# Gathered rows in five slots instead of three, gathers four tile steps ahead, attention steps written out

## The chip, the core and the metric

One NeuronCore of a Trainium2 chip runs the whole program in one launch. The metric is the device time of that launch in microseconds. The core's engines each run their own list of instructions in order and meet at semaphores: TensorE (PE), VectorE (DVE), ScalarE (ACT), GpSimd (POOL) and SyncE (SP). DMAs are issued by SP, ACT and POOL; only POOL issues those with row indices.

## The reference

32 batches of 128 tokens, 512 wide, pass a block of gated cross-attention and a gated mixture of experts.

```python
x = x + tanh(g_xattn) * attention(layernorm(x), ctx, ctx)      # 32 query heads, 8 key heads, depth 16
h = layernorm(x)
logits = tanh(h @ Wg1.T) @ Wg2.T                               # 8 experts
top_idx = top_k(logits, 2); scores = softmax of the two, else 0
out = sum over e of scores[e] * (silu(h @ Wup[e].T + bup[e]) @ Wdown[e].T + bdown[e])
x = x + tanh(g_ffn) * out
```

The output is x, in float32.

## The kernel before, in words

**Attention stage.** A software pipeline over the 32 batches. In step s an engine works on several batches at once: it normalises batch s-1, scores batch s-2, and so on to the placement of batch s-7. The function pipeline runs steps 0 to 11 written out, steps 12 to 23 inside a register loop of each engine (Fori, four steps in an iteration, three iterations), and the rest written out. VectorE's statistics of a new batch (L1055) stand once in each step. At the end of a batch its tokens are ranked within their two experts, and GpSimd scatters the normalised rows by two indirect DMAs (L656) to the experts' regions in DRAM.

**Expert stage.** The scattered rows form 71 tiles of 128 rows, each of one expert (TILES). Tile t passes several tile steps: loaded by ACT's queue (z_s), transposed (L1379), multiplied up (L1398 to L1400), activated, multiplied down (L1410 to L1412), its bias added by VectorE in out_rows (L1112) into one of two buffers y_sb, and stored by SP to expert_out in DRAM (L384). out_rows(t) runs in VectorE's tile step t+4 and waits until the store of tile t-2 has landed.

**Mixing.** A token's output needs two rows of expert_out, from the tiles of its two experts. Batch m is mixed at tile step MIX[m], by a formula: at earliest LAG = 9 steps after the tiles that hold its rows, and 1.5 steps after batch m-1. From batch 24 on these steps are 68, 69, 72, 73, 76, 77, 80, 81; batches 24 and 25 need tiles up to 58, 26 and 27 up to 62, 28 and 29 up to 66, 30 and 31 up to 70, the last. The work on a batch goes in this order:

- GpSimd gathers the batch's rows by two indirect DMAs of 256 KB (gather, L695), first y2 and then y1, into slot m % YRING. Before the first batch of a group of two it waits until the group's tiles are stored (stored_through), and before each gather until the slot's earlier batch is used up.
- ACT scales y2 (L846), VectorE multiplies y1 and adds y2 (L1155), GpSimd adds the sum to the residual r_in (L707), and SP stores the result (L377).
- For the last four batches (LATE) VectorE does all of it (L1128, L1132).

GpSimd's list is written by tile steps, and in step s it first holds the adds of the batches with MIX = s-2 and then the gathers of those with MIX = s+2. Nothing but its waits ties it to the tile steps of other engines. Its list near the end is then: add 24, gather 26, add 25, gather 27, add 26, gather 28, add 27, gather 29, gather 30, gather 31. SP's list has, by tile steps, the store of tile s-4, then the stores of mixed batches with MIX = s-3, then loads of residuals.

Of the kernel before, what the change touches and what calls it, by code (L numbers as in the profile page):

```python
# [51 lines left out]
EPS = 1e-5  # L52
TAB0 = 24
UP = 12582912.0
LOOP1 = 24
O_LOAD, O_NORM, O_S, O_ST, O_OUT, O_GATE, O_ROUTE, O_SLOT = range(8)
STEPS = B + O_SLOT
SOLO = B - 1 + O_GATE
LOOP0 = 12
YRING = 3  # L60
RRING = 5
LAG = 9
RING = 4
# [11 lines left out]
        eng.wait_ge(sem, value)  # L75


def pipeline(eng, step, steps, first, last, unroll):

    for s in range(first):  # L80
        step(s, s % unroll)
    with eng.Fori(0, (last - first) // unroll) as i:
        for u in range(unroll):
            step(i * unroll + (first + u), (first + u) % unroll)
    for s in range(last, steps):
        step(s, s % unroll)


# [24 lines left out]
def mixed_at(s):  # L113

    return [m for m in range(B) if MIX[m] == s]


def block_kernel(nc, x_d, ctx_d, gx_d, gf_d, wg1_d, wg2_d, w_d, bup_d, bdn_d, out_d):
# [5 lines left out]
    with top:  # L124
# [182 lines left out]
        def ring4(b, q, per):  # L307

            return (b - q) * (per // 4) + per
# [6 lines left out]
        @block.sync  # L316
        def _(sp):
            def first_tiles():

                for b in range(SEG[0] - RING, SEG[0]):  # L320
                    sp.wait_ge(scattered[b % RING], ring4(b, b % RING, 32))
                sp.wait_ge(tab_in[0], 32)
                for t in range(RING):
                    row = sp.value_load(tab_r[0:1, t:t + 1], min_val=0, max_val=ROWS - P)
                    sp.dma_start(z_s[t][:, :], slots_d[bass.ds(row, P), :]).then_inc(tile_loaded[t], 16)

            def step(s, u):
                if isinstance(s, int) and s == SOLO:
                    sp.wait_ge(pv_done, 2 * B)
                    sp.wait_ge(on_done, 2 * B)  # L330
                    sp.dma_start(bdn[:, :], bdn_d.to_broadcast([P, E * D])).then_inc(bdn_loaded, 16)
                b, p = s - O_LOAD, (u - O_LOAD) % 2
                if valid(b):
                    wait(sp, n_done, b - 1)
                    sp.dma_start(x_in[p][:, :], x_d[bass.ds(b, 1), :, :].rearrange("a s d -> (a s) d")).then_inc(x_loaded[p], 16)
                    wait(sp, kt_done, b - 1)
                    wait(sp, v_done, b - 1)
                    sp.dma_start(c_in[p][:, :], ctx_d[bass.ds(b, 1), :, :].rearrange("a s d -> (a s) d")).then_inc(c_loaded[p], 16)
                b, p = s - O_OUT, (u - O_OUT) % 2
                if valid(b):  # L340
                    wait(sp, z_done, b - 1)
                    wait(sp, res_stored[p], ring2(b - 2, p))
                    sp.dma_start(x_res[p][:, :], x_d[bass.ds(b, 1), :, :].rearrange("a s d -> (a s) d")).then_inc(res_loaded[p], 16)
                b = s - O_LOAD
                if valid(b):
                    wait(sp, w_lo_done, b)
                    sp.dma_start(wst[:, :], w_d[bass.ds(b, 1), :, :].rearrange("a p n -> (a p) n")).then_inc(w_loaded, 16)
                b, p = s - O_GATE, (u - O_GATE) % 2
                if valid(b):
                    sp.wait_ge(res_done, b + 1)  # L350
                    sp.dma_start(x2_d[bass.ds(b, 1), :, :].rearrange("a s d -> (a s) d"), x_res[p][:, :]).then_inc(res_stored[p], 16)


                if isinstance(s, int) and s == SOLO - 2:
                    sp.wait_ge(w_lo_done, B)
                    sp.wait_ge(n_done, B)
                    sp.wait_ge(kt_done, B)
                    sp.wait_ge(v_done, B)
                    sp.wait_ge(qt_done, B)
                    sp.dma_start(bup[:, :], bup_d.to_broadcast([P, E * HE])).then_inc(bup_loaded, 16)  # L360
                    first_tiles()

            pipeline(sp, step, SOLO + 1, LOOP0, LOOP1, RING)

            def load_residual(m):

                wait(sp, stored[m % RRING], 16 * (m // RRING))
                sp.dma_start(r_in[m % RRING][:, :], x2_d[m:m + 1, :, :].rearrange("a s d -> (a s) d")
                             ).then_inc(r_loaded[m % RRING], 16)

            def store_mixed(m):

                if m < LATE:
                    sp.wait_ge(mix2, m + 1)
                else:
                    sp.wait_ge(late_done, m - LATE + 1)
                sp.dma_start(out_d[m:m + 1, :, :].rearrange("a s d -> (a s) d"), r_in[m % RRING][:, :]  # L377
                             ).then_inc(stored[m % RRING], 16)

            for s in range(TSTEPS):  # L380
                t, p = s - 4, s % 2
                if valid(t, TILES):
                    sp.wait_ge(y_done, t + 1)
                    sp.dma_start(y_d[t * P:(t + 1) * P, :], y_sb[p][:, :]).then_inc(y_stored[p], 16)  # L384
                if s == 5:
                    sp.wait_ge(ends_done, 1)
                    sp.wait_ge(zero_done, 1)
                    _, found = nc.values_load_multi_w_load_instructions(
                        ends[0:1, :], engines=[mybir.EngineType.SP], min_val=0, max_val=ROWS - P,
                        skip_runtime_bounds_check_because="an expert's rows end within its region")  # L390
                    for row in found:
                        sp.dma_start(slots_d[bass.ds(row, P), :], r_in[0][:, :]).then_inc(pads_done, 16)
                if 20 <= s < 20 + RRING:
                    if s == 20:
                        sp.wait_ge(rows_done, 2)
                        scattered_all(sp)
                        sp.wait_ge(pads_done, 16 * E)
                        for b in range(B - 2, B):
                            sp.wait_ge(res_stored[b % 2], ring2(b, b % 2))
                    load_residual(s - 20)  # L400
                for m in mixed_at(s - 3):
                    store_mixed(m)
                for m in mixed_at(s - 6):
                    if m + RRING < B:
                        load_residual(m + RRING)
            for q in range(RRING):
                sp.wait_ge(stored[q], 16 * len(range(q, B, RRING)))

        @block.gpsimd
        def _(pool):  # L410
# [218 lines left out]
            def step(s, u):  # L629
# [10 lines left out]
                if valid(b5):  # L640
                    pool.wait_ge(res_loaded[p5_], ring2(b5, p5_))
                    pool.wait_ge(att_done, 2 * b5 + 2)
                    g.tensor_tensor(x_res[p5_][:, :], x_res[p5_][:, :], z[q5][:, :], ALU.add).then_inc(res_done, 1)  # L643
                    if isinstance(s, int) and TAB0 <= s < TAB0 + 11:
                        if s == TAB0:
                            pool.wait_ge(run_done, SEG[KNOWN - 1])
                        table(0, s - TAB0)
                    pool.wait_ge(o_mv, b5 + 1)
                    g.tensor_tensor(ve_o[:, :], mv_o[:, 1:2], eps[:, :], ALU.add).then_inc(o_ve, 1)
                    pool.wait_ge(o_ve, b5 + 1)  # L650
                    g.tensor_tensor(rs_o[:, :], ve_o[:, :], minus_half[:, :], ALU.pow).then_inc(o_rs, 1)
# [7 lines left out]
                if valid(b0):  # L659
# [2 lines left out]
                    g.tensor_tensor(ve_n[:, :], mv_n[:, 1:2], eps[:, :], ALU.add).then_inc(n_ve, 1)  # L662
                    pool.wait_ge(n_ve, b0 + 1)
                    g.tensor_tensor(rs_n[:, :], ve_n[:, :], minus_half[:, :], ALU.pow).then_inc(n_rs, 1)
                if isinstance(s, int) and s == SOLO:
                    pool.wait_ge(st_done[1], 2 * B)
                    pool.wait_ge(on_done, 2 * B)
                    g.memset(r_in[0][:, :], 0.0).then_inc(zero_done, 1)

            pipeline(pool, step, STEPS, LOOP0, LOOP1, RING)  # L670
            pool.wait_ge(run_done, B)
            for n in range(11):
                table(1, n)
# [27 lines left out]
            for s in range(TSTEPS):  # L701
                for m in mixed_at(s - 2):
                    if m >= LATE:
# [2 lines left out]
                    pool.wait_ge(mix1, m + 1)  # L706
                    g.tensor_tensor(r_in[m % RRING][:, :], r_in[m % RRING][:, :], y1[m % YRING][:, :],  # L707
                                    ALU.add).then_inc(mix2, 1)
                for m in mixed_at(s + 2):
                    if m == 0:  # L710
                        pool.wait_ge(rows_done, 2)
                    if m == 0 or m in SEG:
                        stored_through(tiles_through(level_of(m)))
                    gather(m, level_of(m))

        @block.scalar
        def _(act):
# [79 lines left out]
                    act.wait_ge(w_loaded, 16 * (s + 1))  # L797
                    a.activation(w_hi[:, bass.ds(s * WCHUNK, WCHUNK)], wst[:, :], ACT.Copy).then_inc(w_hi_done, 1)

            pipeline(act, step, SOLO, LOOP0, LOOP1, RING)  # L800

            def hidden(t):

# [65 lines left out]
        def _(dve):  # L869
# [192 lines left out]
                if valid(b6):  # L1062
                    masks(b6, p6_)

            pipeline(dve, step, SOLO, LOOP0, LOOP1, RING)

            expert = {}

# [142 lines left out]
        def _(pe):  # L1211
# [155 lines left out]
                    pe.wait_ge(att_done, 2 * b4 + 1)  # L1367
                    rows_back(b4, 1)

            pipeline(pe, step, SOLO, LOOP0, LOOP1, RING)  # L1370

            expert = {}

# [124 lines left out]
```

## Time and profile before

| | |
|---|---|
| runs shown | 698.03, 698.19, 696.45 us; median 698.03 |
| profiled execution | 695.72 us, of which span 693.9 us |
| TensorE matmul busy | 634.2 us, 91% of the span |
| VectorE busy | 521.6 us, 75% |
| ScalarE busy | 378.3 us, 55% |
| GpSimd busy | 353.8 us, 51% |
| granted TensorE clock, mean | 0.978 |
| moved by DMA | 129.40 MB, mean 186 GB/s |

The attention stage lasts until about 400 us, the expert stage from there to about 675 us, the mixing from about 510 us to the end. Shares of the whole span mix these stages; a stage has to be read by its own stretch, and the chain of waits says which engine's work ended last in it.

### The profile page before, as it was taken

What the parts mean: (1) busy time and instruction counts of PE and PEld (TensorE: products, weight loads), DVE (VectorE), ACT (ScalarE), POOL (GpSimd) and SP (SyncE); (2) the same over time, 40 slices, a digit from 0 to 9 for tenths busy, and PEclk for the clock granted to TensorE, in tenths of its full rate; (3) what the DMA queues carried; (4) which work ended last, traced back from release to release, by engine and by line L of the source; (5) the groups of instructions that cost most, each with busy time, mean ns of one, the idle gap of its engine ahead of it and who ended that gap; (6) DMA issues with size and microseconds to landing.
All of it is one profiled execution on the core that took longest, in us unless ns stands there. A gap on an engine that the chain in (4) does not pass through costs nothing.

```text
span 693.9 us, 17038 instructions
## 1 busy us (share of the span) xinstructions
PE 634.2 (91%) x5064; PEld 432.1 (62%) x5064; DVE 521.6 (75%) x1456; ACT 378.3 (55%) x692; POOL 353.8 (51%) x538
## 2 busy tenths in 40 slices
PE   3779999999999999999999977899999999999970
PEld 2435555555555555555555466789998888888850
DVE  3468888888888888888888455476767788887763
ACT  2267777777767676767676531333334544544430
POOL 4123545464545455656665536890032666575454
PEclk9999999999999999999999989899999999999995
DMA  3123344444444444444432677344665999999977
GB/s 103 53 66 116 114 141 149 139 142 141 144 140 144 140 144 141 145 141 145 143 126 77 208 279 256 109 154 152 215 227 177 304 348 345 348 354 352 334 250 256
DMA packets 65032, 129.40 MB, mean 186 GB/s; under 512 B 8640, under 2 KB 12736, under 8 KB 64704
## 3 DMA queue, kind: packets, MB, share of 16 engines
q1 hardware_dynamic: 44496, 77.35, 32.9%
q0 software_dynamic: 10368, 33.56, 14.3%
q10 hardware_dynamic: 10096, 17.59, 7.8%
q8 instruction: 38, 0.62, 0.4%
q14 instruction: 34, 0.28, 0.1%
HBM read 74.20 MB, written 54.26 MB: 185 GB/s over the span
## 4 chain that ended last, share of the span: by engine, by line
PE 77%; DVE 11%; issue 4%; DMA 2%; POOL 2%; ACT 1%; SPq 1%; DVEq 0%; ACTq 0%; POOLq 0%
PE s_ps L1281 13%; PE bank_a L1260 8%; PE st_ps L1304 8%; DVE nmax L993 7%; PE st_ps L1398 5%; PE st_ps L1399 5%; PE st_ps L1400 5%; PE s_ps L1379 4%; PE bank_c L1221 3%; PE bank_b L1269 3%; PE st_ps L1312 3%; PE bank_q L1356 2%; PE bank_a L1411 2%; PE bank_a L1412 2%; PE bank_a L1410 2%
## 5 line engine op out<-in xcount | busy, mean ns | idle before, releaser
L993 DVE TENSOR_REDUCE nmax<-s_ps 128x8 f32<-128x1024 f32 x128 | 156.4, 1222 | 62.3 <-PE s_ps L1281 61.2
L754 ACT ACTIVATE probs<-st_ps 128x1024 f32<-128x1024 f32 x128 | 131.2, 1025 | 67.2 <-PE st_ps L1312 63.6
L1281 PE MATMUL s_ps<-k_t,q_t 32*128 32x256 f32 x1024 | 151.9, 415 | 17.2 <-DVE nmax L993 14.4
L1304 PE MATMUL st_ps<-q_t,k_t 32*128 32x512 f32 x512 | 145.6, 645 | 0.3
L1281 PEld LDWEIGHTS s_ps<-k_t,q_t 32*128 32x128 f32 x1024 | 92.6, 192 | 68.9 <-DVE nmax L993 44.7
L695 POOL DMA_INDIRECT y<-expert_out,rows_all x64 | 64.6, 1009 | 57.7 <-DMA expert_out<-y_sb 43.3
L1398 PE MATMUL st_ps<-w_hi,zh 128*128 x284 | 86.9, 306 | 1.3 <-DVE zl L1092 1.3
L1399 PE MATMUL st_ps<-w_lo,zh 128*128 x284 | 80.7, 284 | 0.0
L1400 PE MATMUL st_ps<-w_hi,zl 128*128 x284 | 80.5, 283 | 0.0
L831 ACT ACTIVATE t_sb<-u_sb 128x256 f32<-128x256 f32 x71 | 29.7, 418 | 87.1 <-DVE u_sb L1102 78.1
L656 POOL DMA_INDIRECT slots<-z,slot_i x64 | 64.6, 1009 | 16.0 <-issue 15.7
L1260 PE MATMUL bank_a<-probs,v_aug 128*32 128x512 f32 x512 | 68.2, 605 | 0.0
L707 POOL TENSOR_TENSOR r_in<-r_in,y 128x512 f32<-128x512 f32 x28 | 36.4, 1299 | 59.1 <-DVE y L1155 57.1
L1398 PEld LDWEIGHTS st_ps<-w_hi,zh 128*128 128x128 f32 x284 | 55.0, 194 | 1.5 <-issue 1.5
L1399 PEld LDWEIGHTS st_ps<-w_lo,zh 128*128 128x128 f32 x284 | 55.4, 195 | 0.0
L1400 PEld LDWEIGHTS st_ps<-w_hi,zl 128*128 128x128 f32 x284 | 54.8, 193 | 0.0
L1092 DVE TENSOR_TENSOR zl<-s_ps,zh 128x512 fp32r<-128x512 f32 x71 | 49.1, 691 | 5.7 <-ACT zh L814 1.5
L643 POOL TENSOR_TENSOR x_res<-x_res,z 128x512 f32<-128x512 f32 x32 | 40.6, 1267 | 19.3 <-DVE z L892 19.3
L1312 PE MATMUL st_ps<-nm_t,pick 32*128 32x512 bf16 x256 | 49.1, 376 | 0.0
L761 ACT ACTIVATE o_sb<-bank_a 128x512 f32<-128x512 f32 x64 | 38.5, 602 | 16.1 <-PE bank_a L1260 16.1
L1379 PE MATMUL s_ps<-ident_f,z_s 128*128 128x128 f32 x284 | 43.3, 276 | 2.0 <-issue 1.8
L814 ACT ACTIVATE zh<-s_ps 128x512 fp32r<-128x512 f32 x71 | 42.2, 594 | 3.7 <-PE s_ps L1379 2.7
(182 smaller groups left out, 1376.6 us busy)
## 6 DMA issues: line engine op xcount, KB each, us to landing
expert_out<-y_sb SPq DMA_DIRECT2D x71, 256.0 KB, 3.9
z_s<-slots ACTq DMA_DIRECT2D x67, 256.0 KB, 3.9
x_in<-in_x SPq DMA_DIRECT2D x32, 256.0 KB, 2.7
wst<-in_w SPq DMA_DIRECT2D x32, 256.0 KB, 2.6
x_res<-in_x SPq DMA_DIRECT2D x32, 256.0 KB, 2.8
x_scratch<-x_res SPq DMA_DIRECT2D x32, 256.0 KB, 2.0
r_in<-x_scratch SPq DMA_DIRECT2D x32, 256.0 KB, 5.4
out<-r_in SPq DMA_DIRECT2D x32, 256.0 KB, 5.1
```

Of the source, the lines that this page charges most:

```text
L656: g.indirect_dma_start(out=slots_d, out_offset=bass.IndirectOffsetOnAxis(ap=slot_i[q7][:, j:j + 1], axis=0), in_=z[q7][:, :], in_offset=No ...
L695: g.indirect_dma_start(out=y[m % YRING][:, :], out_offset=None, in_=y_d[0:tiles_through(n) * P, :], in_offset=bass.IndirectOffsetOnAxis(ap ...
L754: a.activation(out, st_ps[:, :].rearrange("t (k n) -> t k n", k=2), ACT.Exp, scale=HD ** -0.5).then_inc(exp_done[half], 1)
L993: v.tensor_reduce(out, s_ps[:, :].rearrange("s (r g c t) -> s r g c t", r=2, g=2, c=2), X_AXIS, ALU.max, negate=True).then_inc(max_done, 1)
L1260: last = t_.matmul(bank_a[32 * j:32 * j + 32, :], v_aug[r][:, 32 * k:32 * k + 32], probs[:, k * G * S:(k + 1) * G * S], start=True, stop=True,
L1281: last = t_.matmul(s_ps[:, HALF * rr + 2 * P * gg:HALF * rr + 2 * P * (gg + 1)], q_t[r2][row:row + ROWS32, P * g_:P * (g_ + 1)], k_t[r2][r ...
L1304: t_.matmul(st_ps[:, HALF * rr:HALF * (rr + 1)], k_t[r][row:row + ROWS32, P * i:P * (i + 1)], q_t[r][row:row + ROWS32, :], start=True, sto ...
L1312: last = t_.matmul(st_ps[:, HALF * rr:HALF * (rr + 1)], pick[i][row:row + ROWS32, :], nm_t[p][row:row + ROWS32, :], start=False, stop=True ...
L1379: last = t_.transpose(bank[p][:, P * c:P * c + P], z_s[r][:, P * c:P * c + P], ident_f[:, :])
L1398: t_.matmul(o, zh[p][:, P * c:P * c + P], w_hi[:, cols], start=(c == 0), stop=False)
L1399: t_.matmul(o, zh[p][:, P * c:P * c + P], w_lo[:, cols], start=False, stop=False)
L1400: last = t_.matmul(o, zl[p][:, P * c:P * c + P], w_hi[:, cols], start=False, stop=(c == DC - 1))
```

## The change

YRING goes from 3 to 5, so the gathered rows y1 and y2 have five slots each. Four more buffers of 2 KB a partition are needed, and the scratch for dynamic transfers is set to 8192 bytes a partition. In GpSimd's list a batch's gathers stand in step MIX-4 instead of MIX-2. The register loops of all five engines go: pipeline writes every step out, and tests for a step's number lose their check of its type.

```diff
-LOOP1 = 24
-LOOP0 = 12
-YRING = 3
+YRING = 5
...
-def pipeline(eng, step, steps, first, last, unroll):
-
-    for s in range(first):
-        step(s, s % unroll)
-    with eng.Fori(0, (last - first) // unroll) as i:
-        for u in range(unroll):
-            step(i * unroll + (first + u), (first + u) % unroll)
-    for s in range(last, steps):
+def pipeline(step, steps, unroll):
+
+    for s in range(steps):
         step(s, s % unroll)
...
-            pipeline(pool, step, STEPS, LOOP0, LOOP1, RING)
+            pipeline(step, STEPS, RING)
...
-                for m in mixed_at(s + 2):
+                for m in mixed_at(s + 4):
                     if m == 0:
                         pool.wait_ge(rows_done, 2)
                     if m == 0 or m in SEG:
                         stored_through(tiles_through(level_of(m)))
                     gather(m, level_of(m))
...
-    nc = bacc.Bacc("TRN2", target_bir_lowering=False, num_devices=1)
+    nc = bacc.Bacc("TRN2", target_bir_lowering=False, num_devices=1, dynamic_dma_scratch_size=8192)
```

## Rows read from the trace of the kernel before

**Rows 1.** Timeline of VectorE: start us, us, engine, line, operation, out<-in, count.

```profile
70.67 0.68 DVE L1055 BATCH_NORM_STATS2 st_n<-x_in 128x6 f32<-128x512 f32 x1
...
128.28 0.69 DVE L1055 BATCH_NORM_STATS2 st_n<-x_in 128x6 f32<-128x512 f32 x1
...
279.98 0.68 DVE L1055 BATCH_NORM_STATS2 st_n<-x_in 128x6 f32<-128x512 f32 x1
...
360.63 0.69 DVE L1055 BATCH_NORM_STATS2 st_n<-x_in 128x6 f32<-128x512 f32 x1
```

**Rows 2.** Busy time by stretch: PE, PEld, DVE, ACT, POOL, clock, DMA share, GB/s.

```profile
480.00:500.00 20.00, 20.00 (x142) 18.11 (x142) 14.17 (x33) 7.68 (x18) 0.00 (x0) 1.00 0.60 202
...
560.00:580.00 20.00, 20.00 (x140) 17.92 (x139) 16.27 (x34) 10.21 (x22) 12.45 (x12) 1.00 1.00 343
...
680.00:700.00 20.00, 0.00 (x0) 0.00 (x0) 5.93 (x8) 0.00 (x0) 5.19 (x6) 0.60 0.51 168
```

**Rows 3.** Timeline of VectorE, L1112 (tiles 12, 16, 64, 65).

```profile
472.91 0.68 DVE L1112 SCALAR_TENSOR_TENSOR y_sb<-bank_q,bdn 128x512 f32<-128x512 f32 x1
...
486.68 0.68 DVE L1112 SCALAR_TENSOR_TENSOR y_sb<-bank_q,bdn 128x512 f32<-128x512 f32 x1
...
655.41 0.69 DVE L1112 SCALAR_TENSOR_TENSOR y_sb<-bank_q,bdn 128x512 f32<-128x512 f32 x1
...
659.64 0.69 DVE L1112 SCALAR_TENSOR_TENSOR y_sb<-bank_a,bdn 128x512 f32<-128x512 f32 x1 [0.72 <-DMA expert_out<-y_sb]
```

**Rows 4.** Waits, whole span: who waited for whom, us in total, times, longest us.

```profile
DVE r_in L1128 <- DMA y<-expert_out,rows_all: 7.1, 3, 4.8
...
DVE r_in L1132 <- DMA y<-expert_out,rows_all: 2.7, 3, 1.7
```

**Rows 5.** Chain of waits from 125 to 235 us: start us, us, what.

```profile
132.72 0.89 issue
...
226.48 0.89 issue
```

**Rows 6.** Timeline of GpSimd from 640 us (idle before and its releaser in brackets).

```profile
651.30 0.96 POOL L695 DMA_INDIRECT y<-expert_out,rows_all  x1
...
661.56 1.30 POOL L707 TENSOR_TENSOR r_in<-r_in,y 128x512 f32<-128x512 f32 x1 [5.48 <-DVE y L1155]
...
673.70 1.27 POOL L707 TENSOR_TENSOR r_in<-r_in,y 128x512 f32<-128x512 f32 x1 [4.44 <-DVE y L1155]
...
675.11 1.35 POOL L695 DMA_INDIRECT y<-expert_out,rows_all  x1
...
677.74 1.27 POOL L707 TENSOR_TENSOR r_in<-r_in,y 128x512 f32<-128x512 f32 x1
...
681.67 0.94 POOL L695 DMA_INDIRECT y<-expert_out,rows_all  x1 [0.30 <-issue]
...
685.77 0.95 POOL L695 DMA_INDIRECT y<-expert_out,rows_all  x1 [0.31 <-DVE r_in L1132]
```

**Rows 7.** Timeline of VectorE at the end.

```profile
674.27 0.69 DVE L1112 SCALAR_TENSOR_TENSOR y_sb<-bank_q,bdn 128x512 f32<-128x512 f32 x1 [0.72 <-PE bank_q L1412]
...
674.88 0.74 DVE L1155 SCALAR_TENSOR_TENSOR y<-y,coef 128x512 f32<-128x512 f32 x1
...
690.64 0.75 DVE L1132 SCALAR_TENSOR_TENSOR r_in<-y,coef,r_in 128x512 f32<-128x512 f32 x1 [0.50 <-DMA y<-expert_out,rows_all]
```

**Rows 8.** Timeline of SP's DMA queue at the end.

```profile
672.92 2.39 SPq L384 DMA_DIRECT2D expert_out<-y_sb  x2
```

**Rows 9.** DMA issues of the page: KB each, median us from issue to landing.

```profile
expert_out<-y_sb SPq DMA_DIRECT2D x71, 256.0 KB, 3.9
```

**Rows 10.** Chain of waits from 600 us to the end.

```profile
652.20 6.89 DMA expert_out<-y_sb
...
685.77 4.77 DMA y<-expert_out,rows_all
```

**Rows 11.** Tile expert_out, written by stores and read by gathers.

```profile
DMA to landing us min/median/max: 2.0/4.8/7.2
```

More of the change, by code:

```diff
@@ L327, in step @@
             def step(s, u):
-                if isinstance(s, int) and s == SOLO:
+                if s == SOLO:
                     sp.wait_ge(pv_done, 2 * B)
@@ L351, in step @@
                     sp.dma_start(x2_d[bass.ds(b, 1), :, :].rearrange("a s d -> (a s) d"), x_res[p][:, :]).then_inc(res_stored[p], 16)
-                if isinstance(s, int) and s == SOLO - 2:
+                if s == SOLO - 2:
                     sp.wait_ge(w_lo_done, B)
@@ L361, in step @@
                     first_tiles()
-            pipeline(sp, step, SOLO + 1, LOOP0, LOOP1, RING)
+            pipeline(step, SOLO + 1, RING)
             def load_residual(m):
@@ L643, in step @@
                     g.tensor_tensor(x_res[p5_][:, :], x_res[p5_][:, :], z[q5][:, :], ALU.add).then_inc(res_done, 1)
-                    if isinstance(s, int) and TAB0 <= s < TAB0 + 11:
+                    if TAB0 <= s < TAB0 + 11:
                         if s == TAB0:
@@ L664, in step @@
                     g.tensor_tensor(rs_n[:, :], ve_n[:, :], minus_half[:, :], ALU.pow).then_inc(n_rs, 1)
-                if isinstance(s, int) and s == SOLO:
+                if s == SOLO:
                     pool.wait_ge(st_done[1], 2 * B)
@@ L798, in step @@
                     a.activation(w_hi[:, bass.ds(s * WCHUNK, WCHUNK)], wst[:, :], ACT.Copy).then_inc(w_hi_done, 1)
-            pipeline(act, step, SOLO, LOOP0, LOOP1, RING)
+            pipeline(step, SOLO, RING)
             def hidden(t):
@@ L1063, in step @@
                     masks(b6, p6_)
-            pipeline(dve, step, SOLO, LOOP0, LOOP1, RING)
+            pipeline(step, SOLO, RING)
             expert = {}
@@ L1368, in step @@
                     rows_back(b4, 1)
-            pipeline(pe, step, SOLO, LOOP0, LOOP1, RING)
+            pipeline(step, SOLO, RING)
             expert = {}
```

## The prediction

> **What bounds the kernel now.** I read the busy time by stretch first, then the starts of one instruction that recurs in every step, then the waits, and last the chain with each engine's timeline at the end of the span. Three stages matter.
>
> In the attention stage TensorE and VectorE hand scores and maxima to each other, and a step takes the same time again and again. One mark per step is the statistics instruction of L1055 [rows 1]: from 70.67 to 128.28 there are five steps of 11.52 us; from 279.98 to 360.63 there are seven, again of 11.52 us. Between 128.28 and 279.98 lie 13 steps in 151.70 us. These are the steps that run inside the register loop (steps 12 to 23, and the entry into it). The reader is to see that only there the period is broken.
>
> In the expert stage TensorE is busy for 20.0 us of 20 both where the DMA engines are at 0.60 and where they are at 1.00 [rows 2]. The bias addition that ends a tile (L1112) starts at 472.91 for tile 12 and at 486.68 for tile 16: 3.44 us a tile [rows 3]. The gathers are not what anything waits for here: in the waits the only instructions that wait for gathered rows are the two of the last four batches, L1128 and L1132 [rows 4]. So a deeper look-ahead as such is worth nothing between 510 and 670 us, except through what it does to other transfers.
>
> At the end TensorE has stopped by 675 us, and 19 us follow in which a short chain runs: last tile written, stored, gathered, mixed, stored. In the last stretch VectorE and GpSimd are busy for 5.9 and 5.2 us [rows 2], so the tail is made of waits, and of GpSimd's one queue.
>
> **The change part by part.**
>
> *The loops.* The 13 marked steps took 151.70 us; at the undisturbed 11.521 us they take 149.78. Difference 1.92 us. The chain shows how it looks: pieces of 0.88 to 0.89 us called issue, the first at 132.72 and the last at 226.48, three in all and four steps (46.9 us) apart [rows 5], where the engines come to an iteration's start. Written out, these steps are like those on either side. Those are written out already and run at 11.52, so I take the whole 1.92 as gone. Bounds: 0 if the longer program is fetched no better than the loop was; 1.92 at most. Every later stage starts from this stage's end, so the gain is kept.
>
> *Queue order on GpSimd.* Steps are not clocked: GpSimd runs down its list as fast as waits let it. The batches from 24 on are mixed at steps 68, 69, 72, 73, 76, 77, 80, 81 (from the schedule's formula). With two steps of lead the list ends add 24, gather 26, add 25, gather 27, add 26, gather 28, add 27, gather 29, 30, 31. With four steps it is add 23, gather 26, 27, add 24, add 25, gather 28, 29, add 26, add 27, gather 30, 31. Five slots instead of three are what lets gather m go before add m-3 without waiting for its slot. The trace has the old order [rows 6]: add 24 at 661.56, add 26 at 673.70, gather 28 behind it at 675.11, add 27 at 677.74, then four gathers (29, 30) and the first of batch 30 at 681.67 behind the two of batch 29, the last of 31 at 685.77.
>
> *The tail.* The last tile's y_sb is written from 674.27 to 674.96, the mix of batch 27 ends at 675.62 [rows 7]; the store of that tile is the second of the two SP issues that end at 675.31 [rows 8], so it was issued at about 675.0. A store of this kind lands 3.9 us later in the median [rows 9]: 678.9. That is what gather 30 must have. In the old order it started at 681.67, because gathers 28 and 29 stood before it. In the new order they are long issued, and the queue is free once add 27 is done: 675.62 + 1.27 = 676.9. So gather 30 starts at 678.9, 2.7 us earlier. The three gathers behind it keep their 4.10 us (681.67 to 685.77), the last keeps its 4.77 us to landing [rows 10], the mix (690.64) and the last store keep theirs. Tail: -2.7 us. Bounds by the shortest and the longest landing of these transfers, 2.0 and 7.2 us [rows 11]: 677.0 gives -4.7, 682.2 gives +0.5. I take the median, since the DMA engines have less to do in that stretch once gathers 28 and 29 are out of it.
>
> The Trainium skill ("DMA: Bandwidth & Descriptors", Anatomy of one DMA) puts a GpSimd transfer at about 2.0 us plus its bytes over 436 GB/s, 2.6 us for 256 KB. The last gather's 4.77 us is far from that; by the page the sum would be 2.2 us better, by the trace it stays.
>
> *The wait that moves.* Gather 28 needs tile 66 in memory, and behind that wait now stand adds 26 and 27, and behind those SP's stores of the two batches. Tile 66 is written at 659.64 + 3.44 = 663.1, stored 0.7 later, landed 3.9 later: 667.7. Four gathers at 1.3 us end by 672.9; add 26 started at 673.70 anyway. With 7.2 us to landing they end at 676.2, adds 26 and 27 at 678.7: still before 678.9. Nothing is lost. Gather 26 needs tile 62, written at 655.41 - 2 x 3.44 = 648.5 and landed by 656.1 even at the 6.89 us seen below; add 24, which then stands behind gathers 26 and 27 (5 us), started at 661.56.
>
> *The late store.* One tile step takes 4.23 us (655.41 to 659.64), with 0.72 us of VectorE waiting for a y_sb buffer [rows 3]. The store it waited for took 6.89 us from 652.20 [rows 10]; two steps less the write of the buffer allow 2 x 3.44 - 0.69 = 6.19. Gather 25 was issued at 651.30 [rows 6], just ahead of it. In the new order gather 25 goes one batch earlier, behind add 21 instead of add 22, and the next one not before add 23. I take this 0.72 us as gone; bounds 0 and -0.72, and a loss if a jam forms elsewhere (below).
>
> *Scratch and slots.* Half the scratch for GpSimd's transfers, four more 2 KB buffers: no instruction is added. Cost zero as long as those in flight have room; four are issued within 4.1 us at 4.8 us to landing, so about four are in flight.
>
> Sum: -1.92 - 2.7 - 0.72 = -5.3 us. The profiled execution took 695.72 us (span 693.9 and 1.8 around it): 690.4. The median shown, 698.03, is 2.3 above that execution, and the runs spread from 696.45 to 698.19; the same step from the median gives 692.7 us.
>
> **Rivals.** *The tail does not move.* The last store lands late (7 us), or gather 30 is held otherwise. For it: the stretch is busy with stores and the 7.2 us exist. Against: the gathers of 28 and 29, which ran beside it, are then done before it. Then -1.92 - 0.72 = -2.6: 695.4.
>
> *The halved scratch holds only two transfers.* The third of the last four gathers then waits for the first: 678.9 + 4.77 = 683.7 instead of 678.9 + 2 x 1.37 = 681.6, the last starts at 685.0 and the tail gains 0.7 instead of 2.7: 694.7. In the expert stage four gathers per three tiles (10.3 us) two at a time need 9.6 us and just fit. Nothing in the trace shows a full ring. The Trainium skill ("DMA: Bandwidth & Descriptors", The descriptor swizzle and Terms; "SBUF — State Buffer", SBUF size) gives 9 descriptors of 16 B per side and engine for such a transfer and 16 KiB per partition for the rings. By it 8 KB would hold some 56 transfers, an estimate; so this rival is held small.
>
> *Slower: stores crowded out.* With the DMA engines at 1.00 share [rows 2] more gathers open at once could lengthen the stores of y_sb from 3.9 to the 6.89 us seen once; each such store then holds VectorE and so TensorE for 0.72 us. The loops and the tail give 4.6, so it decides from seven stores on. With 12 of the 35 tiles between 540 and 660 us: +8.6 - 4.6 = +4.0: 702.0. For it: the share, and that it happened once. Against: bytes per tile are unchanged, and GpSimd still issues one batch per add, so the depth grows once, by one batch.
>
> *More than forecast.* From 486.68 to 655.41 there are 48 tile steps in 168.73 us, 3.515 each: 3.6 us above 3.44. If that is contention and goes, -8.9: 689.1. Against: TensorE is busy throughout [rows 2], and no wait for a transfer shows there but the one.
>
> *The written-out steps are fetched slowly.* Only the tail and the store: -3.4, 694.6.
>
> **How the numbers follow.** Forecast 0.58 (own range 690 to 695.5); tail unmoved 0.12; more 0.12; scratch 0.05; stores crowded out 0.08; fetch 0.05. A change under 0.3%, 2.1 us, can't be told from none. Forecast counts 0.55 faster, 0.03 same; tail unmoved (695.4 is on the edge) 0.06 and 0.06; scratch 0.04 and 0.01; fetch 0.04 and 0.01; more 0.12 faster; crowded stores 0.06 slower, 0.02 same. Faster 0.81, same 0.13, slower 0.06. The range leaves out part of "more" and the crowded stores: 688.5 to 697.
>
> **What would show it.** Right: the L1055 starts 11.52 us apart through all steps; on GpSimd gathers 28 and 29 before adds 26 and 27, and the first gather of batch 30 with a wait for a store of expert_out before it, 4 us after the last y_sb; no 0.7 us wait before L1112. Wrong: several waits before L1112 in the expert stage; a gather instruction well over 1.5 us without VectorE beside it (scratch); issue gaps in steps 12 to 23; gather 30 more than 6 us after the last y_sb.

## The result and the profile after

The changed kernel's median is 692.95 us in 9 runs, the kernel before has 696.45 us in the 9 runs beside it: ratio 0.9945, 95% interval [0.9924, 0.9966], 3.5 us between the medians. Timed twice more, on other occasions, it gave 0.9960 [0.9939, 0.9981] and 0.9936 [0.9909, 0.9964]. The forecast was 692.7 us from a base of 698.03; the base has come down by 1.6 us with more runs, and the change is smaller than the 5.3 us of the sum. The time was met by luck: two errors offset each other, and the terms were not all right.

The profiled execution took 694.66 us (span 692.5), the slowest of the nine, so its span is only 1.4 us below that of before. It is read here stage by stage, not as a total.

The attention stage, timeline of VectorE, the same two marks as in [rows 1]:

```profile
128.11 0.68 DVE L1048 BATCH_NORM_STATS2 st_n<-x_in 128x6 f32<-128x512 f32 x1
...
277.91 0.68 DVE L1048 BATCH_NORM_STATS2 st_n<-x_in 128x6 f32<-128x512 f32 x1
```

The 13 steps between them take 149.80 us instead of 151.70. Every step in between is 11.52 or 11.53 us long.

The expert stage, timeline of VectorE, tile 16, then the four writes of y_sb up to tile 65 before which VectorE stood idle (tiles 38, 53, 64, 65), and the last one (as [rows 3] and [rows 7]):

```profile
483.50 0.68 DVE L1105 SCALAR_TENSOR_TENSOR y_sb<-bank_q,bdn 128x512 f32<-128x512 f32 x1
...
560.82 0.69 DVE L1105 SCALAR_TENSOR_TENSOR y_sb<-bank_q,bdn 128x512 f32<-128x512 f32 x1 [0.93 <-PE bank_a L1405]
...
615.13 0.69 DVE L1105 SCALAR_TENSOR_TENSOR y_sb<-bank_a,bdn 128x512 f32<-128x512 f32 x1 [0.82 <-PE bank_q L1405]
...
655.94 0.69 DVE L1105 SCALAR_TENSOR_TENSOR y_sb<-bank_q,bdn 128x512 f32<-128x512 f32 x1 [1.67 <-DMA expert_out<-y_sb]
659.59 0.69 DVE L1105 SCALAR_TENSOR_TENSOR y_sb<-bank_a,bdn 128x512 f32<-128x512 f32 x1 [0.16 <-issue]
...
674.24 0.69 DVE L1105 SCALAR_TENSOR_TENSOR y_sb<-bank_q,bdn 128x512 f32<-128x512 f32 x1 [0.69 <-PE bank_q L1405]
```

The 48 tile steps from 483.50 to 655.94 take 172.44 us; before they took 168.73. Before, one write waited for a buffer, 0.72 us; here three do, 3.42 us together (the 0.16 us at tile 65 are issue: VectorE waited for nothing that the profile shows). In the first two waits the releaser named is a TensorE instruction that belongs to another tile; this write needs its own tile's product and a free buffer, and its own product had ended over 3 us earlier (bank_q near 557.3, the write of tile 38 at 560.82), so the wait is put down to the last store but one of y_sb. The stage begins 3.2 us earlier than before, and the last y_sb is written at 674.24, as late as in [rows 7].

The end, timeline of GpSimd (as [rows 6]):

```profile
656.43 0.96 POOL L688 DMA_INDIRECT y<-expert_out,rows_all  x1
...
664.87 1.30 POOL L700 TENSOR_TENSOR r_in<-r_in,y 128x512 f32<-128x512 f32 x1 [1.87 <-DVE y L1148]
670.74 1.02 POOL L688 DMA_INDIRECT y<-expert_out,rows_all  x1 [4.58 <-issue]
...
674.67 0.94 POOL L688 DMA_INDIRECT y<-expert_out,rows_all  x1 [0.30 <-issue]
675.62 2.49 POOL L700 TENSOR_TENSOR r_in<-r_in,y 128x512 f32<-128x512 f32 x2
680.26 0.96 POOL L688 DMA_INDIRECT y<-expert_out,rows_all  x1 [2.15 <-DMA expert_out<-y_sb]
...
684.39 1.07 POOL L688 DMA_INDIRECT y<-expert_out,rows_all  x1 [0.30 <-issue]
```

The order is the one that was worked out: gathers 28 and 29 (670.74 to 674.67) before adds 26 and 27 (675.62), and gather 30 alone waits, for a store of expert_out. It starts 6.02 us after the last y_sb starts; before it was 7.40 (681.67 - 674.27), forecast 4.6. From the last y_sb's start to the end of the span it is 18.26 us, before 19.63. Two of the prediction's own signs of being wrong are there: several waits before L1105 (L1112 before), and gather 30 more than 6 us after the last y_sb.

### The profile page after: what moved, and what is told of

The parts are those of the page before. It is cut to its first block, busy times and chain, and to the rows that moved or that the text cites. A ratio compares the mean times of both kernels' runs of the same rounds, so it can differ in the third digit from the quotient of the medians.

```text
span 692.5 us, 16517 instructions
## 1 busy us (share of the span) xinstructions
PE 631.8 (91%) x5064; PEld 431.8 (62%) x5064; DVE 522.9 (76%) x1456; ACT 377.9 (55%) x692; POOL 352.1 (51%) x538
## 4 chain that ended last, share of the span: by engine, by line
PE 81%; DVE 9%; DMA 3%; issue 3%; ACT 1%; POOL 1%; SPq 1%; ACTq 1%; DVEq 0%; POOLq 0%
PE s_ps L1274 14%; PE bank_a L1253 9%; PE st_ps L1297 8%; DVE nmax L986 7%; PE st_ps L1391 5%; PE st_ps L1393 5%; PE st_ps L1392 5%; PE bank_c L1214 4%; PE s_ps L1372 4%; PE st_ps L1305 3%; PE bank_b L1262 3%; PE bank_q L1349 2%; PE bank_q L1403 2%; PE bank_q L1404 2%; PE bank_q L1405 2%
```

## The experiments

The question was why the expert stage took longer in this profile. Theory 1: the deeper gathers make the stores of y_sb late, which was the prediction's slower rival. Rivals: the longer program's fetches, or chance, that is, a ring of two y_sb buffers that is short in any order.

Read in each profile: S, the 13 steps of the attention stage; E, the 48 tile steps from 16 to 64; H, the idle time before the writes of y_sb of tiles 16 to 68, in sum (0.16 us of it is issue, no wait for a buffer, in before, after, e3, f1 and g2); G, the first gather of batch 30 after the start of the last y_sb; T, from there to the end of the span. Before: S 151.70, E 168.73, H 0.88, G 7.40, T 19.63. Changed: 149.80, 172.44, 3.58, 6.02, 18.26.

**The loops alone (e1, again g1).**

```diff
-YRING = 5
+YRING = 3
...
-                for m in mixed_at(s + 4):
+                for m in mixed_at(s + 2):
...
-    nc = bacc.Bacc("TRN2", target_bir_lowering=False, num_devices=1, dynamic_dma_scratch_size=8192)
+    nc = bacc.Bacc("TRN2", target_bir_lowering=False, num_devices=1)
```

> The attention steps written out, gathers and slots as before. Theory 1 (the loss in the expert stage comes from the deeper gathers): the loops' 1.9 us and nothing else, about 694.5 us against 696.45 of before, the 48 tile steps from tile 16 to 64 in some 168.7 us as before, at most one wait of about 0.7 us before a write of y_sb. Rival (the loss comes from the longer program or its fetches): those 48 steps take over 170 us, several waits before y_sb, and the gain is under 1 us.

> The written-out attention steps alone once more, beside the change on one chip. If the loops' 1.9 us reach the end, 1 to 3 us below before (0.27%); if something later takes them back, no difference.

Ratios 0.9989 [0.9967, 1.0011] and 0.9974 [0.9945, 1.0003]. S 149.79 and 149.82, T 19.50 and 20.14, G 7.39 and 7.37: the loops give 1.9 us in their stage and the end is that of before; in the whole time the ratios make it 0.8 and 1.8 us. H was 1.00 in the first and 3.47 in the second, E 169.93 and 171.97. The longest wait of the second, timeline of VectorE:

```profile
586.04 0.69 DVE L1105 SCALAR_TENSOR_TENSOR y_sb<-bank_q,bdn 128x512 f32<-128x512 f32 x1 [1.50 <-DMA expert_out<-y_sb]
```

So as many waits can come up with the old lead. Theory 1, that the deeper gathers make the stores late, had seemed borne out by the first of the two profiles; the second does not bear it out.

**The gathers alone (e2).** The kernel before with five slots, lead 4 and 8 KB scratch, loops kept.

```diff
-YRING = 3
+YRING = 5
...
-                for m in mixed_at(s + 2):
+                for m in mixed_at(s + 4):
```

> Loops kept; five slots, four steps of lead and the 8 KB scratch as in the change. Theory 1: the tail's 1.4 us is won and some 2.7 us are lost in waits for y_sb buffers, so 695 to 698 us, no clear difference, with three or more such waits of 0.7 to 1.7 us. Rival (the forecast's terms): tail -2.7 and late store -0.7, 693 us, with none.

Ratio 0.9987 [0.9962, 1.0013]; S 151.67, E 169.91, H 3.20, G 5.69, T 17.62. The end is 2 us shorter, three waits for y_sb of 0.33 to 1.17 us behind tile 28 and one of 0.77 at tile 27 stand against it, as expected by theory 1; but g1 has as many without the deeper gathers.

**Four steps of lead for the last batches alone (e3).**

```diff
-                for m in mixed_at(s + 4):
+                for m in [m for d in (2, 4) for m in mixed_at(s + d) if d == (4 if m >= LATE else 2)]:
```

> As the changed kernel, but four steps of lead for the last four batches alone, two for batches 0 to 27. Theory 1: the expert stage is as before (at most one wait before y_sb, 48 tile steps in about 168.7 us), loops -1.9 and tail -1.4 to -2.7 stay: 691.5 to 693 us, about 1 us or more below the changed kernel. Rival (the lead costs nothing, the waits for y_sb are chance): no difference from the changed kernel, 693 us, with as many waits.

Ratio 0.9988 [0.9964, 1.0012]: against both expectations, no better than the loops alone. G 5.88 and T 17.78 are those of the change, S 149.79; but H is 2.54, with waits of 0.42 and 1.54 at tiles 36 and 37 and 0.42 at tile 53, where its gathers had the old lead. That does not bear out theory 1 either. Why its median does not show the end's gain is not settled.

**Four buffers for y_sb (e4, again f2).** The change, with y_sb and its semaphores by tile modulo 4, the scratch at 4 KB.

```diff
+YSB = 4
...
-y_stored = [sem(f"y_stored{i}") for i in range(2)]
+y_stored = [sem(f"y_stored{i}") for i in range(YSB)]
...
-                wait(dve, y_stored[p], ring2(t - 2, p))
+                y = t % YSB
+                wait(dve, y_stored[y], 16 * (t // YSB))
...
-dynamic_dma_scratch_size=8192
+dynamic_dma_scratch_size=4096
```

> As the changed kernel with four buffers for y_sb instead of two, and the scratch for dynamic transfers halved again to 4 KB to make room. Theory 1: a store may take 13 us before it holds VectorE, the 3.4 us of waits before y_sb go, 689.5 to 690.5 us. Rival (TensorE loses the time elsewhere, in fetches or loads of z_s): no better than the changed kernel, 693 us. If the scratch holds too few transfers: gather instructions of mean over 1.2 us instead of 0.99, and slower than the changed kernel.

> Four buffers for y_sb and 4 KB scratch on top of the change, once more: 6 us below before, no waits before y_sb; 2.5 to 3.5 us below the changed kernel if the waits are its cost, as far as it if they are not.

Ratios 0.9906 [0.9880, 0.9931] and 0.9930 [0.9903, 0.9956], the fastest version of all. H is 0 in both, E 168.57 and 168.96. Timeline of VectorE in the first, tiles 16 and 64:

```profile
483.54 0.68 DVE L1109 SCALAR_TENSOR_TENSOR y_sb<-bank_q,bdn 128x512 f32<-128x512 f32 x1
...
652.11 0.68 DVE L1109 SCALAR_TENSOR_TENSOR y_sb<-bank_q,bdn 128x512 f32<-128x512 f32 x1
```

So the time that the expert stage lost in the changed kernel's profile, 172.44 - 168.57 = 3.9 us, goes with the waits for y_sb buffers. The scratch, now a quarter of what it was, does not lengthen the gathers' instructions: a gather instruction takes 997 and 999 ns, in the changed kernel 994, before 1009 (groups by line, GpSimd):

```profile
L691 POOL DMA_INDIRECT y<-expert_out,rows_all x64 | 63.8, 997 | 65.9 <-DMA expert_out<-y_sb 43.4 <-issue 20.4 <-DVE y L1152 0.3
```

**Four buffers with the old lead (f3)**, as e4, but three slots in use.

```diff
-YRING = 5
+YRING = 3
...
-                for m in mixed_at(s + 4):
+                for m in mixed_at(s + 2):
```

> Loops written out, four buffers for y_sb, 4 KB scratch, but three slots in use and two steps of lead as before the change. Theory 1 (lead gains at the end and costs by stores that are late): without the cost of stores this kernel still lacks the tail's gain, so it is 1.4 to 2.7 us slower than the one with four steps of lead: 3 to 4 us below before; the first gather of batch 30 starts 10 to 12 us after the last y_sb starts and behind those of batch 29. Rival (the lead is worth nothing, buffers are all): equal to the one with four steps, 6 us below before.

Ratio 0.9943 [0.9919, 0.9967], beside 0.9930 with four steps. H 0, E 168.74, G 7.41, T 19.96: the end is that of before, with gather 30 behind the gathers of batch 29, though 7.41 us after the last y_sb and not the 10 to 12 expected. The difference of the two ratios, 0.9 us, lies within their intervals, so this run does not decide between theory 1 and its rival.

**Four buffers in the kernel before (g4)**, its loops and lead kept, the edits of e4 for y_sb and 4 KB scratch.

```diff
+YSB = 4
...
-                wait(dve, y_stored[p], ring2(t - 2, p))
+                y = t % YSB
+                wait(dve, y_stored[y], 16 * (t // YSB))
```

> The kernel before, loops and lead as they were, with four buffers for y_sb and 4 KB scratch. If waits for y_sb cost both kernels alike (0.9 us and up in a profile, more in other executions), about 2 us below before and no such waits; if only the deeper gathers bring them, no more than 0.7 us below.

Ratio 0.9974 [0.9949, 0.9999], 1.8 us; H 0, E 169.52, G 7.39, T 19.41. So the waits cost the kernel before something too; the interval goes from 0.1 to 3.6 us.

**The last store by ScalarE's queue (f4).** As e4, tile 70's store issued by ScalarE.

```diff
-                if valid(t, TILES):
+                if valid(t, TILES - 1):
...
+                if s == TILES + 3:
+                    act.wait_ge(y_done, TILES)
+                    act.dma_start(y_d[(TILES - 1) * P:TILES * P, :], y_sb[(TILES - 1) % YSB][:, :]
+                                  ).then_inc(y_stored[(TILES - 1) % YSB], 16)
```

> As four buffers with the change, but the store of the last tile is issued by ScalarE's queue instead of SP's. If that store takes 5 to 6 us to land because it stands behind out and r_in transfers in SP's queue, it lands in 3 to 4 us there, gather 30 starts 2 us earlier and the whole is 1.5 to 2 us less. If the DMA engines themselves are the limit, it lands no earlier and the time stays.

Ratio 0.9920 [0.9896, 0.9945], beside 0.9930 of e4's second run: no gain. Timelines of ScalarE's queue and of GpSimd:

```profile
675.18 0.38 ACTq L862 DMA_DIRECT2D expert_out<-y_sb  x1
```

```profile
682.04 0.96 POOL L691 DMA_INDIRECT y<-expert_out,rows_all  x1 [4.83 <-issue]
```

6.9 us lie between the store's issue and gather 30; the list of DMA issues has the store land after 6.0 us, in f2, where SP issues it, after 4.7. A queue of its own did not make the store land sooner.

**Less beside the last store (g3).** The change, with short results.

```diff
+                n = 16 if LATE - 4 <= m < LATE else P
-                sp.dma_start(out_d[m:m + 1, :, :].rearrange("a s d -> (a s) d"), r_in[m % RRING][:, :]
+                sp.dma_start(out_d[m:m + 1, 0:n, :].rearrange("a s d -> (a s) d"), r_in[m % RRING][0:n, :]
```

> The change, but the results of batches 24 to 27 are stored for 16 of 128 tokens alone (7/8 of those four outputs are left out). If the store of the last tile is late because it shares the DMA engines with them, gather 30 starts about 5 us after the last y_sb starts instead of 5.7 to 6.2, and the time falls by 1 us or so. If not, gather 30 stays at 5.7 to 6.2 us.

The chain of waits in that kernel's last stretch:

```profile
673.97 2.89 DMA expert_out<-y_sb
...
679.64 5.19 DMA y<-expert_out,rows_all
```

The last store now lands in 2.89 us, G is 3.88 and T 15.75, against 5.69 to 6.02 and 17.5 to 18.3 in the changed kernel's three profiles and e2's and e3's. The gathers of batches 28 and 29 are hardly what made the difference: the last of them was issued 3.3 us before this store and 3.2 us before that of f2, which with full results took 4.7 us. So the results stored beside it are a part of what makes the last store late. The time did not fall with it: 0.9935 [0.9903, 0.9966], as the change beside it; this run's profile has waits for y_sb of 2.27 us and the interval is some 4 us wide, so 1 to 2 us can hide in it.

**The change again (f1, g2).**

> The changed kernel once more, beside the other three. If its gain (3.5 us of the median when it was first timed) is the loops' 1.9 us and a tail of 1.4 us less what the waits for y_sb take, it varies with the number of those waits: 0 to 5 us below before, the median some 2 to 3.5 below. If it is the forecast's sum, 5.3 us below.

> The change once more. Loops 1.9 and tail 1.6 us as the profiles so far have them give 3.5 us below before, 1.6 us below the loops alone.

0.9960 and 0.9936 (intervals above). S 149.80 in both, G 5.78 and 5.81, T 17.74 and 17.54, E 169.28 and 168.77, H 1.08 and 0.16. The changed kernel, too, can pass the expert stage without a wait for a buffer. Beside g2, on the same chip, the loops alone (g1) stand at 0.9974: the gathers are worth about 2.6 us there, with intervals that overlap. Timelines of the second, VectorE and GpSimd:

```profile
671.76 0.69 DVE L1105 SCALAR_TENSOR_TENSOR y_sb<-bank_q,bdn 128x512 f32<-128x512 f32 x1 [0.69 <-PE bank_q L1405]
```

```profile
677.57 0.95 POOL L688 DMA_INDIRECT y<-expert_out,rows_all  x1 [2.42 <-DMA expert_out<-y_sb]
```

## Why the prediction was right or wrong

**The loops, -1.92: right.** S fell by 1.90 in the changed kernel and stands at 149.79 to 149.83 in every kernel whose steps are written out, at 151.67 and 151.73 in the two that kept the loops. None of these steps pays for a longer program. That the whole gain reaches the end is not shown; the loops alone timed at 0.8 and 1.8 us, each with an interval that holds 0 and 1.9.

**The order on GpSimd: right**, row for row. The wait that moved did hold something: tile 66 was written at 663.05, its store took 5.9 us to land and not 3.9, gather 28 began at 670.74 and not at 667.7, and add 26 began at 675.62, 1.9 us later than in [rows 6]. As bounded, it cost nothing: adds 26 and 27 ended at 678.1, and gather 30 waited for its own store until 680.26.

**The tail, -2.7: the path right, the landing of the last store wrong.** Gather 30 waits for that store alone, as forecast. It starts 1.4 to 1.7 us earlier after the last y_sb, not 2.7 (G 5.69 to 6.02 in the five profiles with the new lead and two buffers, before 7.40). The mean of T over the five profiles with the old lead (before, e1, g1, f3, g4) is 19.73 us, over the eight with the new one (after, e2, e3, e4, f1, f2, f4, g2) 18.03: -1.7 us; in the kernels with two buffers for y_sb it is 19.76 and 17.79, -2.0, in those with four 19.69 and 18.43, -1.3 (G there 6.22 to 7.58). The step that failed is the store's landing, put at the 3.9 us of [rows 9]. That is the median of all 71 stores, and 24 of the tiles were written before the first gather. In the stretch of mixing the same trace has 5.0; here is the answer for the stores from 535 to 655 us of the kernel before, the row that should have been read:

```profile
L384 SPq DMA_DIRECT2D expert_out<-y_sb x34: 319/320/320, 536.0 to 652.2; - x34
...
DMA to landing us min/median/max: 3.3/5.0/6.9
```

With 5.0 the term comes out as -1.7. The reason given for the median, that the DMA engines have less to do once gathers 28 and 29 are out, was the wrong way round, and with it the argument against the first rival, that these gathers ran beside the last store. In the kernel before they are issued just after that store (from 675.11); in the changed kernel they are issued before it (670.74 to 674.67), took 5.4 to 6.0 us to land and were all still in flight when it started. The store's line among the DMA issues from 674.9 us on, first before, then changed (KB, us to landing):

```profile
expert_out<-y_sb SPq DMA_DIRECT2D x1, 256.0 KB, 2.4
```

```profile
expert_out<-y_sb SPq DMA_DIRECT2D x1, 256.0 KB, 5.0
```

It is so in all profiles that give this landing: 2.0 to 2.4 us in the five with the old lead, where gathers 26 and 27 have landed (f3 does not give the landing of one) and gather 28 is only just being issued, and 4.7 to 6.0 in the six with the new lead and full results (after, e3, f1, f2, f4, g2), where two to four of the gathers of batches 28 and 29 are still in flight. So the new order itself slows the store on which its gain hangs; the results stored beside it add to that, as g3 shows with 2.89 us. The bound of 2.0 to 7.2 held it.

**The late store, -0.72: wrong as a certainty.** A new order of gathers was to remove the one wait for a y_sb buffer; in the changed kernel's first profile there were three, 3.42 us. The rival of crowded stores seemed to have come true. The other profiles do not bear it out: H is 0.88, 1.00, 3.47 (before, e1, g1) and 2.54 (e3, in whose middle the lead is the old one) without the lead, and 3.58, 3.20, 1.08, 0.16 with it, 2.0 in the mean of either four. With four profiles a side that run from 0.2 to 3.6, an effect of the new order of about 1 us, either way, is not excluded. Two buffers leave a store 6.19 us, as the prediction worked out; the stores' median is 4.8 to 5.5 in this stretch in every profile that gives it, with either lead, the slowest 6.4 to 8.1, so some executions meet it often and some never. One wait in one profile said little of the order. What the runs show is that the wait goes with more buffers: 1.8 us in the kernel before (g4), and 2.1 us under the change (f2 against f1, timed together; their intervals overlap).

**Scratch and slots, 0: right.** A quarter of the scratch did not lengthen a gather instruction: in e4 the four gathers of batches 28 and 29 started 1.25 us apart (664.47 to 668.23) while single ones took up to 7.3 us to land. The rival that only two fit falls; how many do, no run shows.

**More than forecast: not seen.** Where no write of y_sb waits (e4, f2, f3, f4, g4), the 48 tile steps still take 168.0 to 169.5 us. So the 3.6 us above 48 x 3.44 are not these waits, and the change does not take them away.

**The sum.** 1.9 + 2.0 + 0 = 3.9 us, measured 3.5; 2.8 and 4.5 by the two later ratios.

**Left open.** The change's stage before the first tile was 0.9 us shorter (last mark to the first y_sb: 59.19 us, before 60.06); the kernels spread from 59.15 to 60.07 here without regard to the change. Executions of one kernel differ by up to 10 us (g1 from 691.65 to 701.35), and the waits for y_sb are not the main part of it: with four buffers f2 goes from 689.60 to 698.00. A part lies at the start: the first of the two marks stands between 127.91 and 131.79 us in the fourteen profiles. In the two latest, g4 and f4, the granted clock was 0.50 from 40 to 44 us, the lower of its two levels (1.2 GHz), where e4 has 1.00, and the step then under way took 14.1 us, in e4 11.3. TensorE had been busy for 2.4 of the 4 us before, in e4 for 2.3; why the clock fell in these executions is not shown.

## What to carry to other kernels

A duration that hangs on contention is to be taken from a stretch with the same neighbours as in the new order, not from the whole run's median; moving transfers forward also moves them beside others. A ring of two whose slack (6.2 us) is little above the median landing (5.0) costs a different amount in each execution, from nothing to over 3 us here, so one profile says little about its change; more buffers took these waits away, and the memory for them lay in a scratch area that the traffic did not need. Where a queue's order is written out, writing down both lists before the run shows which waits move; how long they last has to be read from loaded stretches.

## What was not expected of the hardware

The same 256 KB store, the last one, landed in 2.0 to 2.4 us where the gathers before it had landed, in 2.89 us beside gathers and short results (g3), and in 4.7 to 6.0 us beside two to four gathers and full results. Issued by ScalarE's queue instead of SP's it took 6.0 us (f4): a queue of another engine did not help it.
